# Which engine adds the bias to the keys and takes them out of PSUM in the projection stage

## The reference

```python
xn = (x - mean(x)) / sqrt(var(x) + 1e-5)                  # per row of 128
q, k, v = xn @ Wq + bq, xn @ Wk + bk, xn @ Wv + bv        # 16 heads of 8
qp, kp = relu(q @ rw) + 1e-6, relu(k @ rw) + 1e-6         # per head, 64 features
out = (qp @ (kp^T v)) / (qp . sum(kp) + 1e-6)             # per head and batch
attn = out @ Wo + bo
logits = xn @ wr + br                                     # 8 experts
e = argmax(softmax(logits)); gate = p1 / (p1 + p2)
ffn = gate * (gelu(xn @ w1[e] + b1[e]) @ w2[e] + b2[e])
result = x + attn + ffn
```

## Time and profile before

| what | value |
|---|---|
| median of 3 runs | 228.54 us (228.49 to 228.83) |
| the profiled execution: time | 229.5 us |
| the profiled execution: span of the engines' work | 227.5 us |
| TensorE busy | 198.3 us (87% of the span) |
| VectorE busy | 130.9 us (58%) |
| ScalarE busy | 124.0 us (55%) |
| GpSimd busy | 141.7 us (62%) |
| granted TensorE clock, mean | 0.979 |

### The profile page before, as it was taken

How to read it: one execution, slowest core, us unless ns; L and a number is a source line. 1 busy time by engine, 2 the same in 40 slices (tenths; PEclk the granted TensorE clock), 3 DMA queues, 4 the chain that set the end, 5 groups by cost and what they waited for, 6 DMA issues and landing times. The chain is left out here.

```text
span 227.5 us, 6689 instructions
## 1 busy us (share of the span) xinstructions
PE 198.3 (87%) x2267; PEld 159.3 (70%) x2267; DVE 130.9 (58%) x420; ACT 124.0 (55%) x293; POOL 141.7 (62%) x165
## 2 busy tenths in 40 slices
PE   0399899589999999999999999999999999999930
PEld 0256466456666666666666666999999999999930
DVE  5737735959876667665665575345544455444420
ACT  3167797345654455544555565856666666666600
POOL 1847863022267777777777711018888888888885
PEclk9999999969999999999999999999999999999995
DMA  4945999950011111111112654168999999999331
GB/s 128 286 127 150 200 132 288 303 133 1 4 38 60 55 48 43 58 61 58 54 58 69 201 128 146 48 214 166 179 205 204 211 210 200 211 205 208 58 35 9
DMA packets 32191, 29.53 MB, mean 130 GB/s; under 512 B 5504, under 2 KB 24480, under 8 KB 32160
## 3 DMA queue, kind: packets, MB, share of 16 engines
q1 hardware_dynamic: 24752, 24.14, 40.6%
q0 software_dynamic: 6640, 4.24, 13.7%
q10 hardware_dynamic: 768, 0.74, 1.1%
HBM read 20.17 MB, written 11.49 MB: 139 GB/s over the span
## 5 line engine op out<-in xcount | busy, mean ns | idle before, releaser
L397 POOL DMA_INDIRECT out<-k_all,slots_all x39 | 61.0, 1563 | 25.4 <-DVE k_all L938 18.4
L715 ACT ACTIVATE q_all<-feat,w_slot 128x128 f32<-128x128 f32 x156 | 44.6, 369 | 28.4 <-PE feat L563 17.1
L372 POOL DMA_INDIRECT sorted_x<-rows_all,place_i x32 | 31.7, 990 | 15.6 <-PE kv_bank L471 8.4
L563 PE MATMUL feat<-v_all,w_slot 128*128 128x128 f32 x312 | 41.3, 275 | 0.0
L563 PEld LDWEIGHTS feat<-v_all,w_slot 128*128 128x128 f32 x312 | 38.0, 192 | 0.1
L672 ACT ACTIVATE k_feat<-feat 128x1024 f32<-128x1024 f32 x16 | 16.4, 1025 | 28.0 <-PE feat L449 28.0
L861 DVE TENSOR_SCALAR q_feat<-feat 128x1024 f32<-128x1024 f32 x16 | 19.6, 1225 | 16.2 <-PE feat L460 16.1
L679 ACT ACTIVATE q_feat<-feat 128x1024 f32<-128x1024 f32 x16 | 16.4, 1026 | 19.0 <-PE feat L460 19.0
L328 POOL TENSOR_SCALAR rows_all<-x_all,meanvar,rstd 128x128 f32<-128x128 f32 x23 | 18.7, 822 | 11.7 <-DVE rstd L747 11.7
L854 DVE TENSOR_SCALAR k_feat<-feat 128x1024 f32<-128x1024 f32 x16 | 19.6, 1224 | 10.6 <-PE feat L449 10.6
L460 PE MATMUL feat<-q_all,rw_bd 32*128 32x256 f32 x256 | 19.0, 411 | 7.4 <-DVE k_feat L854 7.4
(11 more groups left out here) (118 smaller groups left out, 313.0 us busy)
## 6 DMA issues: line engine op xcount, KB each, us to landing
w_slot<-w1x SPq DMA_DIRECT2D x39, 258.0 KB
sorted_x<-ones_f SPq DMA_DIRECT2D x1, 2535.0 KB, 17.6
x_all<-in_x SPq DMA_DIRECT2D x8, 256.0 KB, 3.8
w1x<-in_w SPq DMA_DIRECT2D x1, 2048.0 KB, 24.2
out<-res SPq DMA_DIRECT2D x16, 128.0 KB, 1.7
slots_all<-sorted_x SPq DMA_DIRECT2D x23, 65.0 KB
out<-k_all,slots_all POOLq DMA_INDIRECT x39
slots_all<-sorted_x SPq DMA_DIRECT2D x1, 520.0 KB, 5.8
```

The source lines that it names most:

```text
L372: pool.indirect_dma_start(sorted_x, bass.IndirectOffsetOnAxis(ap=place_i[:, t:t + 1], axis=0), rows_all[:, t, :], None).then_inc(x_moved, 16)
L397: pool.indirect_dma_start(out_rows, bass.IndirectOffsetOnAxis(ap=slot_rows[j % SLOT_RING][:, D + 1:XW].bitcast(I32), axis=0), y_sb[j % Y_R ...
L563: ins = pe.matmul(bank[:, a * P:(a + 1) * P], w1_slot[j % W1_RING][:, a * P:(a + 1) * P], xsT[j % X_RING][:, :], start=True, stop=True)
L715: act.activation(hidden_T[j % H_RING][:, a * P:(a + 1) * P], hid_bank[j % HID][:, a * P:(a + 1) * P], ACT.Gelu, bias=w1_slot[j % W1_RING][ ...
```

## The change

ScalarE keeps `save_q(c)` and no longer takes out the keys. VectorE gets `save_k(c)`: wait for the keys of chunk c, then one `tensor_scalar` that adds the bias column to the 128x512 result in PSUM and writes it to `k_all`. It stands in VectorE's loop behind `row_stats`, `row_scale` and `normalise` of chunk c+3 and ahead of `find_top` and `pick`. The semaphore `qk_saved` becomes two, `q_saved` and `k_saved`: TensorE waits for the first ahead of the query matmul, for the second ahead of the key matmul, and for both in full ahead of the attention stage. VectorE waits once for the six weight loads ahead of its loop, because the bias column comes with them. The diff in full:

```diff
--- before.py
+++ after.py
@@ -188,7 +188,7 @@
         stats_ready, mv_ready, std_ready, rstd_ready = sem("stats_ready"), sem("mv_ready"), sem("std_ready"), sem("rstd_ready")
         xn_ready, xn_dve = sem("xn_ready"), sem("xn_dve")
         xnT_ps, xnT_ready = sem("xnT_ps"), sem("xnT_ready")
-        qk_ps, qk_saved = sem("qk_ps"), sem("qk_saved")
+        qk_ps, q_saved, k_saved = sem("qk_ps"), sem("q_saved"), sem("k_saved")
         v_ps, v_saved = sem("v_ps"), sem("v_saved")
         v_spread = sem("v_spread")
         x_biased = sem("x_biased")
@@ -419,8 +419,9 @@
             def project(c):
                 s = c % 2
                 pe.wait_ge(xnT_ready, c + 1)
-                due(pe, qk_saved, 2 * c - 2)
+                due(pe, q_saved, c - 1)
                 pe.matmul(q_bank[s], wq_sb[:, :], xnT[s][:, :], start=True, stop=True).then_inc(qk_ps, 1)
+                due(pe, k_saved, c - 1)
                 pe.matmul(k_bank[s], wk_sb[:, :], xnT[s][:, :], start=True, stop=True).then_inc(qk_ps, 1)
                 for h in range(CB):
                     due(pe, v_saved, 2 * c - 1 + h)
@@ -514,7 +515,8 @@
                 ins.then_inc(wo_ps, 1)
 
             pe.wait_ge(rw_in, 16 * H)
-            pe.wait_ge(qk_saved, 2 * CHUNKS)
+            pe.wait_ge(q_saved, CHUNKS)
+            pe.wait_ge(k_saved, CHUNKS)
             for i in range(NBATCH):
                 k_features(i)
                 if i == 1:
@@ -631,10 +633,9 @@
                 due(act, v_ps, 2 * c - 2)
                 act.activation(xnT[c % 2][:, :], xnT_bank[c % 2], ACT.Copy).then_inc(xnT_ready, 1)
 
-            def save_qk(c, n):
-                bank, bias, dst = ((q_bank, bq_col, q_all), (k_bank, bk_col, k_all))[n]
-                act.wait_ge(qk_ps, 2 * c + n + 1)
-                act.activation(dst[:, c * CN:(c + 1) * CN], bank[c % 2], ACT.Identity, bias=bias[:, 0:1]).then_inc(qk_saved, 1)
+            def save_q(c):
+                act.wait_ge(qk_ps, 2 * c + 1)
+                act.activation(q_all[:, c * CN:(c + 1) * CN], q_bank[c % 2], ACT.Identity, bias=bq_col[:, 0:1]).then_inc(q_saved, 1)
 
             def save_v(c, h):
                 act.wait_ge(v_ps, 2 * c + h + 1)
@@ -656,8 +657,7 @@
             for c in range(CHUNKS):
                 if c + 1 < CHUNKS:
                     save_xnT(c + 1)
-                save_qk(c, 0)
-                save_qk(c, 1)
+                save_q(c)
                 if c == CHUNKS - 3:
                     act.activation(warm[:, :], ln_eps[:, :], ACT.Exp)
                 for h in range(CB):
@@ -777,6 +777,10 @@
                 then(dve.tensor_tensor(onehot[:, :, ts].rearrange("p e t -> p t e"), is_top[:, :, :],
                                        strided(top_w[:, 0:1], [(1, RT), (0, E)]), ALU.is_equal))
 
+            def save_k(c):
+                dve.wait_ge(qk_ps, 2 * c + 2)
+                dve.tensor_scalar(k_all[:, c * CN:(c + 1) * CN], k_bank[c % 2], bk_col[:, 0:1], None, ALU.add).then_inc(k_saved, 1)
+
             def normalise(c):
                 dve.wait_ge(rstd_ready, c + 1)
                 for t in range(c * CT + NORM[c], (c + 1) * CT):
@@ -796,11 +800,13 @@
                 row_stats(c)
                 row_scale(c)
                 normalise(c)
+            dve.wait_ge(wts_in, 16 * 6)
             for c in range(CHUNKS):
                 if c + 3 < CHUNKS:
                     row_stats(c + 3)
                     row_scale(c + 3)
                     normalise(c + 3)
+                save_k(c)
                 if c % 2 == 1:
                     find_top(c // 2)
                     if c + 1 < CHUNKS:
```

## The result

The changed kernel took 232.17 us (median of 4 runs, 231.46 to 232.36), the kernel before 228.51 us (228.49 to 228.83, 4 runs) beside it: ratio 1.0151, 95% interval 1.0128 to 1.0174, 3.66 us between the medians. Forecast were 230.1 us and a range to 231.0. The direction was right and the size was not. Its executions fall into two groups, 2.4 us apart, and these four all belong to the upper one; with two later series of 12 and 6 runs there are 9 executions from 229.24 to 230.23 (mean 229.6) and 13 from 231.33 to 233.26 (mean 232.0). The kernel before shows no such gap: in the two series beside them it ran 61 times, from 227.10 to 229.51, mean 228.6. The lower group lies inside the range that was forecast, the upper one outside.

The account below looks back on a forecast made before the run. TensorE paces the stage, and its stalls ahead of chunks 5 and 7 begin on VectorE. Three uncovered evictions less slack, 3 x 0.61 - 0.27 = +1.56 us on the 228.54 median, give 230.1 us, range 229.1 to 231.0.

Parts of the forecast that it names:

- the carrying of the sum to the time of the run: After the stage: the 1.56 us reaches the end unchanged; 231.06 on the profiled execution, 230.1 on the median, lower by 0.96.
- rival 3: Attention stage: starting later, it has no step down of TensorE's clock, so the kernel is not slower; chance 0.07.
- The term for VectorE: Chunk stage: three evictions at 0.61 us uncovered on VectorE, less 0.27 of slack at chunk 6, +1.56 us.
- keys 0: Chunk 0's key eviction, ahead of chunk 4's statistics: hidden by ScalarE's values, 0.39 us to spare.
- Keys 1: Chunk 1's key eviction, ahead of find_top(0): delays TensorE's transposes of chunk 5 by 0.61 us, gap 1.64.
- Keys 2: Chunk 2's key eviction, ahead of chunk 6's statistics: root 0.95 us late after 0.27 slack, hidden from TensorE by GpSimd's timing.
- Keys 3: Chunk 3's key eviction, ahead of find_top(1): chunk 7's transposes 1.56 us late in all, gap from 0.40 to 1.35.
- Keys 4 to 6: Key evictions of chunks 4 to 6: free, where VectorE waits for values anyway and no statistics are left.
- rival 1: Chunk stage: only one eviction counts, slack handed out anew at chunk 6; 0.61 to 0.9 us, 229.15 to 229.45; chance 0.10.
- ScalarE as the hidden gate (2): Roots of chunks 4 and 6: ScalarE's shorter queue brings them forward, worth at most 0.35 us, 229.75; chance 0.05.
- Rival 4: Pauses ahead of chunks 5 and 7: one more step down of the clock, 1.7 us, 231.8; chance 0.06.
- Rival 5: Chunk stage: VectorE's evictions hidden wholly in its idle time, no effect, 228.5; chance 0.08 together with gains.

Follow-up runs that it names:

- keys_last: Changed kernel, but VectorE takes out only the keys of chunks 4 to 7 and ScalarE keeps 0 to 3; ratio 1.0006 to the kernel before.
- keys_odd: Changed kernel, but VectorE takes out only the keys of chunks 1, 3, 5 and 7; stage +1.05 us, ratio 1.0108 to the kernel before.
- after_again: The changed kernel run again unchanged, against the kernel before: 230.11 us over 12 runs, ratio 1.0071.
- before_shift: Kernel before, plus 20 idle matmuls and a wait for the last values ahead of the attention stage on TensorE; 229.98 us, ratio 1.0092.

## Why the prediction was wrong, point by point

**The step that failed** is the carrying of the sum to the time of the run. The sum has nothing ahead of chunk 2 and nothing behind the stage ("After the stage nothing runs by its own clock"), and it took the step down for one that always comes (no step down is rival 3, with a chance of 0.07). The runs showed that both of TensorE's clock steps differ between executions of one program: the step up came at 13.3 or 14.6 us in the kernel before, at 14.7 or 16.3 in the changed one, and the step down came in one profile and not in another. The prediction read the profile from 13.20 us on and never asked why the matmuls of chunk 0 ahead of it were nearly twice as long as those of chunk 1 (queries 1.91 us, against 1.02). So it had no term for the 1.51 us that the first profile shows ahead of chunk 2. And it took 0.96 us off to pass from the profiled execution to the median. On the profiled execution itself the account closes: 229.5 + 1.51 + 1.71 = 232.7, measured 232.36. The kernel before hardly ever has the step down outside that first profile; the four measured first of the changed kernel (mean clock 0.979 to 0.980) all had it. That these four all fell into the upper group, when 13 of 22 do in all, was chance as far as the record shows. A range that had taken in the late step up beside the step down, 1.5 us, would have reached 231.6, still short of the median measured first. What decides the moment of the step up stays open.

**The term for VectorE** was right in mechanism and a little small. Predicted 3 x 0.61 - 0.27 = 1.56; with the measured 0.66 it is 1.71, and measured are 1.65 in the stage, 1.71 to the features. What was mis-sized is the eviction: the straight line gave a record of 0.69 and a step of 0.61; measured 0.75 and 0.66, just over the upper bound of 0.65. The 0.69 in the upper bound of the sum, 3 x 0.69 - 0.27 + 0.13, stands for an eviction that costs its whole record; no run shows that. In its place the runs showed a cost of 0.66 at a record of 0.75: the next start comes 0.09 us ahead of the record's end, as it did in the earlier trace rows.

**By its steps:** keys 0 hidden: yes, the root of chunk 4 stood behind ScalarE's values still. Keys 1 uncovered: yes, the root of chunk 5 came 2.15 us later, 1.51 of it from the start. Keys 2 less 0.27 of slack, GpSimd hiding it at chunk 6: yes, TensorE's transposes of chunk 6 waited for nothing. Keys 3 uncovered: yes, gap 1.41 where 1.35 was forecast; ahead of chunk 5 it was 1.54 for 1.64. Keys 4 to 6 free: shown by `keys_last`. Keys 7: 0.06 longer on VectorE than on ScalarE, where the prediction had them equal. TensorE waited ahead of no key matmul. GpSimd's normalising of chunk 6, beside keys 3 and more of VectorE's work, took 2.60 us for three tiles in place of 2.41, and nothing came of it. One small miss more, which the prediction had not looked at: the transposes of chunk 4 come 0.12 us later against chunk 2 than before. GpSimd's normalising of chunk 4 took 2.60 us in place of 2.48 beside keys 1 and `find_top(0)`, and TensorE was close behind it (its end at 23.31, the transposes at 23.36). These 0.12 us were spent there, so the gap ahead of chunk 5 is the smaller one.

**The rivals:** one eviction only (rival 1) is ruled out by `keys_odd`, 1.05. ScalarE as the hidden gate (2): taking work off ScalarE moved no root forward. Rival 3, no step down because the attention stage starts later and so no slower kernel, is half seen in the lower group: the profile of `after_again` has no step down. Without it that group was cheaper, and the kernel was slower all the same, since the earlier trace rows was hardly ever the state of the kernel before either. Against its 228.6 the mean of the lower group, 229.6, is 1.0 us more, less than the 1.7 of the lengths; how early these executions stepped up is known for the profiled one alone, so the rest of that stays open. Rival 4, one more step down of 3.73 x 0.46 = 1.7 us in the pauses ahead of chunks 5 and 7 (231.8), was near in size and wrong in place: none came there, though they grew to 1.54 and 1.41 us; the granted clock is 1.00 from 16.50 to 42.00. Rival 5 falls with all of it. The chances, 0.85 for slower, stand.

## What to carry to other kernels

Ask which engine begins the chain at the stalls, not which engine is fullest: VectorE had 11 us to give in the average and only 0.36 us of waiting in each of the two places where TensorE stood still, and the same eight evictions cost 1.65, 0.32 or 0.12 us in the stage by their place in its queue (the last at the price of 1.6 us behind it). Before costing an edit against a single profile, look at the matmul durations of the very first work and at each stretch with a lowered clock, take both as terms that can change from one execution to the next, and take many runs: four of them here all told of the same group. The mean granted clock of each execution tells at once whether a profile is of the usual kind: here it was 0.979 in the one that the prediction read, and 0.984 to 0.992 in 83 of 85 later ones.

## What the runs showed that I had not expected

Starting the attention stage 1.8 us later on TensorE, behind 20 idle matmuls and with no other engine's work changed, splits the times of this kernel in two groups about 2 us apart (`before_shift`), while the kernel before has none of these gaps. And 48 idle matmuls ahead of the first real one, 5 us in which TensorE had nothing to do, with 16 more behind the transposes of chunk 0, make the kernel 0.53% shorter (0.9947, 0.9921 to 0.9972): the transposes of chunk 0 take 0.66 in place of 1.09 us and the keys of chunk 0 take 1.02 in place of 1.14.
